# Dividing attention outputs ahead of the output weights instead of behind them, in a two-layer decoder on one core

## The reference, cut to what matters

```
attn = jax.nn.softmax(logits, axis=-1)
out = jnp.einsum('bhnm,bhme->bnhe', attn, v)
...
return jnp.dot(out, Wp) + bp
```

## Time and profile before

| | |
|---|---|
| median of 3 runs | 4618.46 us (4615.41 to 4620.7) |
| the profiled execution's own time, and its span | 4600.18 us, 4598.4 us |
| busy: PE, PEld | 4301.6 us (94%), 2382.7 us (52%) |
| busy: DVE, ACT, POOL | 2227.8 us (48%), 1803.9 us (39%), 3141.8 us (68%) |
| mean granted TensorE clock | 0.960 of 2.4 GHz |

### The profile page before, as it was taken

How to read it: one execution, slowest core, us unless ns; L and a number is a source line. 1 busy time by engine, 2 the same in 40 slices (tenths; PEclk the granted TensorE clock), 3 DMA queues, 4 the chain that set the end, 5 groups by cost and what they waited for, 6 DMA issues and landing times. The chain is left out here.

```text
span 4598.4 us, 69354 instructions
## 1 busy us (share of the span) xinstructions
PE 4301.6 (94%) x25904; PEld 2382.7 (52%) x25904; DVE 2227.8 (48%) x2764; ACT 1803.9 (39%) x2082; POOL 3141.8 (68%) x1379
## 2 busy tenths in 40 slices
PE   7999799999999999999999968599899999999968
PEld 3555455555555555555555446244455555555436
DVE  4555655555454555555455112456565545455212
ACT  2333244444444444444444422133234444444422
POOL 3556279989898988989899930000048989899950
PEclk9999899999999999999999979799779999999979
DMA  1000000000000000000000001100000000000001
GB/s 34 5 5 2 4 2 1 2 2 2 2 2 2 2 2 2 3 2 2 2 1 2 1 17 46 40 9 12 4 1 2 2 2 1 1 1 2 1 12 30
DMA packets 30387, 30.95 MB, mean 7 GB/s; under 512 B 6929, under 2 KB 22786, under 8 KB 30082
## 3 DMA queue, kind: packets, MB, share of 16 engines
q1 hardware_dynamic: 28626, 24.39, 1.8%
q10 hardware_dynamic: 1456, 2.46, 0.2%
HBM read 23.17 MB, written 3.67 MB: 6 GB/s over the span
## 5 line engine op out<-in xcount | busy, mean ns | idle before, releaser
L410 POOL TENSOR_TENSOR c_SUM<-c_SUM,c_PR 128x1024 f32<-128x1024 f32 (+1 forms) x1176 | 2792.9, 2375 | 263.9 <-ACT c_PR L490 158.7
L568 DVE TENSOR_REDUCE c_MX<-c_XB 128x2 f32<-128x1024 f32 (+2 forms) x1156 | 1394.3, 1206 | 1224.0 <-PE c_XB L690 1223.0
L490 ACT ACTIVATE c_PR<-c_S 128x1024 f32<-128x1024 f32 (+1 forms) x1224 | 1194.7, 1023 | 1694.9 <-PE c_S L735 1579.8
L753 PE MATMUL c_O<-c_PR,c_V 128*64 128x512 f32 (+1 forms) x4896 | 1197.0, 607 | 2.8 <-ACT c_PR L490 2.8
L753 PEld LDWEIGHTS c_O<-c_PR,c_V 128*64 128x64 f32 (+1 forms) x4896 | 294.0, 136 | 568.4 <-issue 394.1
L735 PE MATMUL c_S<-c_SH,c_ONE 64*128 64x512 f32 x2448 | 482.0, 389 | 0.0
L490 ACT ACTIVATE a_PR<-a_S 128x1024 f32<-128x1024 f32 x256 | 248.7, 1022 | 444.9 <-PE a_S L735 444.9
L568 DVE TENSOR_REDUCE a_MX<-a_XB 128x2 f32<-128x1024 f32 x246 | 301.2, 1224 | 188.0 <-PE a_XB L690 96.6
L690 PE MATMUL c_XB<-c_KHM,c_QH 64*128 64x512 f32 x1632 | 369.5, 448 | 11.7 <-DVE c_MX L568 7.7
L735 PE MATMUL c_S<-c_QH,c_KHM 64*128 64x512 f32 x1728 | 348.3, 399 | 8.5 <-ACT c_PR L490 8.4
L735 PE MATMUL c_S<-c_QH,c_KLM 64*128 64x512 f32 x1728 | 341.5, 391 | 0.0
(11 more groups left out here) (209 smaller groups left out, 4352.7 us busy)
## 6 DMA issues: line engine op xcount, KB each, us to landing
f_W<-in_L_w SPq DMA_DIRECT2D x34, 256.0 KB, 2.7
CTX<-in_ctx ACTq DMA_DIRECT2D x12, 192.0 KB, 4.4
a_KS<-scratch_k SPq DMA_DIRECT2D x16, 96.0 KB
a_QS<-scratch_q SPq DMA_DIRECT2D x16, 96.0 KB
scratch_q<-rot_qh SPq DMA_DIRECT2D x2, 512.0 KB, 4.6
scratch_k<-rot_kh SPq DMA_DIRECT2D x2, 512.0 KB, 6.2
c_WQ<-in_L_xattn_Wq SPq DMA_DIRECT2D x12, 64.0 KB, 1.8
c_WO<-in_L_xattn_Wo SPq DMA_DIRECT2D x12, 64.0 KB, 1.8
```

The lines of the kernel that those rows point to most:

```text
L410: pool.tensor_tensor(out[0:kp], out[0:kp], tile[0:kp], ALU.add).then_inc(summed, 1)
L490: act.activation(PR[u % BUFS][0:kp, :, :].rearrange("p h q -> p (h q)"), S[u % 2][0:kp, :], ACT.Exp)\
L568: dve.tensor_reduce(MX[:, q:q + tiles, :, column], bank[:].rearrange("p (h k) -> p h k", h=2) [:, :, 0:tiles * m].rearrange("p h (q k) -> ...
L753: last = pe.matmul(O[ROWS[h], :], V[pair.par][0:kp, t, ROWS[h]], PR[u % BUFS][0:kp, h, :], start=t == 0, stop=t == TILES - 1)
```

## The change

D is now made in the layout of the outputs, in which each partition is one dimension of one head and each column a query: the product of a block of ones with SUM gives every one of the head's 64 partitions the sum of its 512 queries (128x512 in all; in a1 one product with a matrix that has ones in the two rows that hold denominators). VectorE takes the reciprocal of all 512 columns, in four quarters of 128 columns (`divide`, two quarters in D's own group and two in the next), and multiplies OT with it in place (`normalise`). Y is then one job for both heads: four products over all 128 rows, and one addition of 128x512 to X. M is made with the transposing form of the product. In a0, K of the second chunk and Q move behind D; the tables keep Y two groups or more behind D.

```diff
-                g = 2
-                for job in [("D", 1 - half), ("YA", 1 - half), ("YB", 1 - half)] + jobs:
+                for job, g in [(("D", 1 - half), 2), (("Y", 1 - half), 5)] + [(job, 2) for job in jobs]:
...
-                self.side[half] = {(2, 0): ("D", 1 - half), (2, 1): ("YA", 1 - half), (3, 0): ("YB", 1 - half),
-                                   (3, 1): ("M", 1 - half)}
+                self.side[half] = {(1, 0): ("D", 1 - half), (3, 0): ("Y", 1 - half), (3, 1): ("M", 1 - half)}
...
-            self.side[0] = {(0, 0): ("Q", 0), (0, 1): ("K", 0), (1, 0): ("K", 1), (1, 1): ("D", 1), (2, 0): ("YA", 1),
-                            (2, 1): ("YB", 1), (3, 0): ("Q", 1), (3, 1): ("M", 1)}
-            self.side[1] = {(0, 0): ("V", 0), (1, 0): ("V", 1), (1, 1): ("D", 0), (2, 0): ("YA", 0), (2, 1): ("YB", 0),
-                            (3, 1): ("M", 0)}
+            self.side[0] = {(0, 0): ("Q", 0), (0, 1): ("K", 0), (1, 0): ("D", 1), (2, 0): ("K", 1), (2, 1): ("Q", 1),
+                            (3, 0): ("Y", 1), (3, 1): ("M", 1)}
+            self.side[1] = {(0, 0): ("V", 0), (1, 0): ("D", 0), (2, 0): ("V", 1), (3, 0): ("Y", 0), (3, 1): ("M", 0)}
...
+        self.division = [{job: at for at, job in side.items()}["D", 1 - half][0] for half, side in enumerate(self.side)]
...
-        RDEN = sb("RDEN", [P, 8])
+        RDEN = sb("RDEN", [P, HALF])
...
-                def output(half, ps, h, n):
+                def output(half, n):
 
                     dve.wait_ge(side_free, n)
-                    last = None
-                    for t in range(4):
-                        xt = X[:, 4 * half + t, :]
-                        last = dve.scalar_tensor_tensor(xt, ps[:, t * D:(t + 1) * D], RDEN[:, 2 * t + h:2 * t + h + 1],
-                                                        xt, ALU.mult, ALU.add)
-                    last.then_inc(side_free, 1)
+                    xt = X[:, 4 * half:4 * half + 4, :].rearrange("p t d -> p (t d)")
+                    dve.tensor_tensor(xt, SIDE[:], xt, ALU.add).then_inc(side_free, 1)
+
+                def divide(pair, half, parts, end=False):
+
+                    n = plan.job(pair.p, ("D", half), end)
+                    for i in parts:
+                        if i == 0:
+                            dve.wait_ge(side_done, n + 1)
+                        q = slice(i * P, (i + 1) * P)
...
+                        each = dve.reciprocal(RDEN[:, q], SIDE[:, q])
+                        if i == 3:
+                            each.then_inc(side_free, 1)
+
+                def normalise(pair, half, end=False):
...
+                    dve.wait_ge(side_free, plan.job(pair.p, ("D", half), end) + 1)
+                    dve.wait_ge(evac, 2 * to.p + half + 1)
+                    dve.tensor_tensor(OT[:], OT[:], RDEN[:], ALU.mult).then_inc(normal, 1)
...
-                        dve.reciprocal(RDEN[:], SIDE[:, 0:8]).then_inc(side_free, 1)
...
+                            after = group - plan.division[half]
                             maxima(0)
+                            if after == 1:
+                                divide(pair, 1 - half, (2, 3), end)
                             if group == GROUPS - 1 and not (end and half):
                                 shift(plan.maximum(pair.p, half, plan.half_maxima))
                             maxima(1)
+                            if after == 0:
+                                divide(pair, 1 - half, (0, 1), end)
+                            if after == 1:
+                                normalise(pair, 1 - half, end)
                             for job in side_jobs(half, group, 0, end):
...
                 def denominators(half):
+
+                    if packed is not None:
+                        return pe.matmul(SIDE[:], ones[:], OT[:], start=True, stop=True)
+                    last = None
+                    for h in range(2):
+                        last = pe.matmul(SIDE[ROWS[h], :], ones[:, ROWS[h]], SUM[half][:, h, :], start=True, stop=True)
+                    return last
+
+                def outputs():
                     last = None
                     for t in range(4):
-                        q = slice(t * P, (t + 1) * P)
-                        if packed is not None:
-                            last = pe.matmul(SIDE[:, 2 * t:2 * t + 2], OT[:, q], ones[:], start=True, stop=True)
-                            continue
-                        for h in range(2):
-                            last = pe.matmul(SIDE[:, 2 * t + h:2 * t + h + 1], SUM[half][:, h, q], ones[:, 0:1],
-                                             start=True, stop=True)
-                    return last
-
-                def outputs(h):
-                    last = None
-                    for t in range(4):
-                        last = pe.matmul(SIDE[:, t * D:(t + 1) * D], OT[ROWS[h], t * P:(t + 1) * P], WO[ROWS[h], :],
-                                         start=True, stop=True)
+                        last = pe.matmul(SIDE[:, t * D:(t + 1) * D], OT[:, t * P:(t + 1) * P], WO[:], start=True, stop=True)
                     return last
...
-                            last = pe.matmul(SIDE[:, t * P:(t + 1) * P], NM[:, t, :, :].rearrange("p h e -> p (h e)"),
-                                             ident[:], start=True, stop=True)
+                            last = pe.transpose(SIDE[:, t * P:(t + 1) * P], NM[:, t, :, :].rearrange("p h e -> p (h e)"),
+                                                ident[:])
...
-                        pe.wait_ge(evac, 2 * to.p + job[1] + 1)
+                        pe.wait_ge(normal, 2 * to.p + job[1] + 1)
```

More of the change, by code:

```diff
@@ L234, in of_pair @@
                 return pair.next()
-            return pair.back() if job[0] in ("D", "YA", "YB") and job[1] == 1 else pair
+            return pair.back() if job[0] in "DY" and job[1] == 1 else pair
         def absent(pair, job):
-            return pair is not None and pair.first and job[0] in ("D", "YA", "YB") and job[1] == 1
+            return pair is not None and pair.first and job[0] in "DY" and job[1] == 1
         def side_jobs(half, group, place, end):
@@ L334, in period @@
                     if not pair.first:
-                        sp.wait_ge(side_done, plan.job(pair.p, ("YB", 1)) + 1)
+                        sp.wait_ge(side_done, plan.job(pair.p, ("Y", 1)) + 1)
                         load_o(pair.p)
@@ L356, in _ @@
                 period(pair_at(pairs - 2), False)
-                sp.wait_ge(side_done, plan.job(pairs - 1, ("YB", 1), True) + 1)
+                sp.wait_ge(side_done, plan.job(pairs - 1, ("Y", 1), True) + 1)
                 load_o(pairs - 1)
@@ L535, in side @@
                     to = of_pair(pair, job)
-                    if kind == "V":
+                    if kind in "VD":
                         return
@@ L561, in side @@
                             dve.wait_ge(bias_added, 1)
-                        output(job[1], SIDE, "YA YB".split().index(kind), n)
+                        output(job[1], n)
                 def maximum(n, bank, unit):
@@ L605, in _ @@
                 dve.wait_ge(side_done, n + 1)
-                dve.reciprocal(RDEN[:], SIDE[:, 0:8]).then_inc(side_free, 1)
-                for h in range(2):
-                    dve.wait_ge(side_done, n + 2 + h)
-                    output(1, SIDE, h, n + 1 + h)
+                dve.reciprocal(RDEN[:], SIDE[:]).then_inc(side_free, 1)
+                dve.wait_ge(side_free, n + 1)
+                dve.wait_ge(evac, 2 * pairs)
+                dve.tensor_tensor(OT[:], OT[:], RDEN[:], ALU.mult).then_inc(normal, 1)
+                dve.wait_ge(side_done, n + 2)
+                output(1, n + 1)
             @block.tensor
@@ L814, in _ @@
                 pe.wait_ge(wo_in, 16 * pairs)
-                for h in range(2):
-                    pe.wait_ge(side_free, n + 1 + h)
-                    outputs(h).then_inc(side_done, 1)
+                pe.wait_ge(normal, 2 * pairs)
+                pe.wait_ge(side_free, n + 1)
+                outputs().then_inc(side_done, 1)
 class NormSemaphores:
```

28 lines of the change are left out of this document (19 added, 9 removed).

## The result

The changed kernel takes 4536.84 us (median of 4 runs, 4533.21 to 4538.78), the kernel before 4617.07 us in the same comparison: a ratio of 0.9824 with a 95% interval of 0.9807 to 0.9841, or 80 us less. The prediction was 4562 us, with a range of 4515 to 4610 us.

The account below looks back on a forecast made before the run. TensorE's own work, and every wait given to it, was taken as the bound. Gains of 15 us (c0, c1), 27 (a0), 13 (a1) and none at the ends, together 56, gave 4618.46 - 56 = 4562 us, range 4515 to 4610.

Parts of the forecast that it names:

- D: On TensorE, two overlapping products of 0.93 us replace sixteen short instructions of 1.87 us: 0.94 us gained a half pass.
- M: On TensorE, four transposing instructions replace eight at about 0.11 us each: 0.44 us gained a half pass.
- Y: On TensorE, one job of 1.08 us replaces YA and YB: gain 0.78 us in a0 and a1, 0.68 in c0 and c1.
- The reciprocal: On VectorE, 6.1 ns a column: 0.94 us a quarter, 3.3 us for all 512 columns.
- The dear case: Rival: reciprocal 1.16 us or more a quarter, SIDE's stall 1.8 us; 24 us gained, 4594 us. Chance 0.17.
- the cheap one: Rival: reciprocal 0.34 us a quarter, no SIDE stall beyond 0.1, none on XB; 119 us gained, 4499 us. Chance 0.14.
- The stall on SIDE: The next V or K behind D in c0, c1 and a0 waits 1.2 us for the reciprocal, 1.3 with the restart.
- XB in a1: Group 3's maximum product in a1 waits 0.8 us; net 0.9 us gained each, 15 times, 13 us.
- a0: First halves (K, Q) gain 2.1 us each, second halves (V) 1.5, the last 2 us: together 27 us.
- The ends: At the four ends, where nothing is beside, c0's 10.4 us from D to last addition becomes about 10: no change.
- The base: The profiled execution of the kernel before, 4600.18 us, is 18 us below the runs' median, so 4618.46 us was the base.
- the falls would come with each stall: Rival: TensorE's clock falls to 1.2 GHz in each new stall, 3.4 us each, 170 us lost, 4732 us. Chance 0.05.

Follow-up runs that it names:

- run 8: D's two products made twice in a row in a0, c0 and c1 of the changed kernel: 4546.77 us, ratio to the kernel before 0.987.
- run 2: The changed kernel with M made by products with the identity again, eight instructions in place of four: 4534.47 us, ratio to the kernel before 0.9836.
- run 11: The kernel of run 10 with M made by products with the identity: 4534.75 us, ratio to the kernel before 0.9828.
- late V: The changed kernel with V behind D one place later in c0 and c1 (K was not moved): 4530.55 us, ratio to the kernel before 0.9828.
- run 4: The changed kernel with plain copies in place of the reciprocal's quarters in the loops, leaving out the division: 4495.97 us, ratio to the kernel before 0.9751.
- run 9: The changed kernel with the reciprocal's quarters spread over VectorE's free slots, and D, V and K moved: 4606.38 us, ratio to the kernel before 0.9987.
- run 3: The kernel before with M's transposes as the only edit: 4588.61 us against 4609.72, ratio 0.9944.
- run 1: The kernel before, unedited, with a second profile: 4616.94 us, ratio 1.0; the profiled execution took 4617.98 us.
- run 12: The changed kernel with a copy of RDEN into OT in place of the multiplication in the loops: 4520.53 us, ratio to the kernel before 0.9801.
- run 6: The changed kernel with V behind D one place later in c0 and c1, and K or V ahead of D in a0: 4522.51 us, ratio to before 0.9813.
- run 10: The kernel of run 6 with a1's reciprocal quarters spread two, one, one: 4508.21 us, ratio to the kernel before 0.9778.

## Why the prediction was right, and where its sizes were off

- **D.** Predicted 0.93 us for two heads, a gain of 0.94. The trace has 0.91, doubling it costs 0.86 to 0.89 in three kinds of half pass (run 8). Shown. a1's D took 1.06 as against 1.
- **M.** Predicted 0.44 us a half pass. Undoing it costs 0.5 in every kind of half pass (runs 2 and 11), some 27 us over all of them; M holds TensorE for 0.59 us in place of 1.09. The Trainium skill's factor of four for FP32 (TensorE: Matmul & The Clock Gate, Terms) would make it 0.66 by the prediction's 0.11 us an instruction; the chip did half the instructions of the same length.
- **Y.** Predicted 1.08 us, a gain of 0.68 in c0 and c1; it held TensorE for 1.09. Read from the trace, not tested by itself.
- **The reciprocal.** Predicted 0.94 us a quarter and 3.3 for 512 columns; 0.89 to 0.96 and 3.36. The dear case is out, and so is the cheap one: the 512 columns took 6.6 ns each with all that is fixed. The Trainium skill's repeat count of 8 (VectorE: DVE Perf Modes, First, the fixed hardware budget), read as eight cycles a column at 0.96 GHz, would be 8.3 ns, an estimate from that page; the measurement does not bear out this reading.
- **The stall on SIDE.** This is the term that was mis-sized. "It now waits 1.2 us" and 1.3 with the restart; in the V halves of c0 it was 0.98, and taking it away gave 0.85 (late V) or 0.6 to 1.1 us (copies). The restart was not there: V's row is 1.15 us behind the wait and 1.16 without one. Counted from D's end (1085.60), the job was due at 4.4 us, as predicted, but the last quarter ended at 5.27 in place of 5.55, because two quarters take 1.76 us together. With the terms as measured a V half comes out right: 0.96 (D) + 0.67 (Y) + 0.50 (M) - 0.98 = 1.15 us, against 1.1. In the K halves the 0.91 us stall costs nearly nothing by itself: run 4 took it away and gained 0.1 us, because K's low part then holds the maximum product for 0.8 us. The prediction named a late reader of SIDE ("SIDE's next reader is pushed late enough to hold the maximum product behind it") as what would make it wrong. In the changed kernel it is just not that late: no wait for it shows in a K half of c0. That both halves gained the same 1.1 us is in part luck, since the wait that would take the stall's place had no term.
- **XB in a1.** Predicted 0.8 us; it was 0.38, and worth 0.44 (runs 4 and 9). Half passes gained 1.35 in place of 0.9, 20 us in place of 13.
- **a0.** Predicted 1.5 (V) and 2.1 (K, Q); it was 2.2 and 2.4. The new waits were 0.91 us for K and 0.73 for Q (1.3 and 0.6 predicted) and 0.93 for V (1.3). Some 0.2 us of the rest are not assigned to a term. Besides, four short falls of the clock in a0 before (half passes of 30.9, 30.7 and 30.7 us where 29.1 is usual, and one of 27.9 where 26.3 is) did not occur after: 6.5 us that no term had. They were also absent with M's transposes alone (run 3) and in run 2, so no single edit is shown to be the cause.
- **Sum.** Predicted 27 + 15 + 13 us; the stages gave 40, 13 and 20. In c0 and c1 the 1.1 us would be 22; the two half passes at the turns of c0's loop took 16.5 us more than usual, 10.4 of them in the four stops and the rest at a lower clock, where before's took 5.6, with 3.5 in two stops. The prediction read its price of a fall of the clock, 3.4 us, from the first of these two; 1.7 of it is a stop for which the profile names nothing.
- **The ends.** Predicted no change; c0's took 10.4 us from D to the last addition and takes 9.0 now, though the clock is low in both.
- **The base.** The profile of before was treated as 18 us below the median for all stages alike. It was one stretch, c0's lead, with a mean clock of 0.86 where run 1 has 0.60; the changed kernel's profile has 0.63. That the falls would come with each stall was rightly given little; that a stretch without any edit moves by 10 to 13.5 us with the clock was not foreseen.

The prediction was short by 24 us of the timed 80. Between run 1's profile and after's it is 26 of 82: 14 in a0 (6.5 of them its falls of the clock), 7 in a1, 7 in c0's lead, and c0 and c1 together 2 the other way, some 10 us more by the sizes of the terms and 12 lost at the loop's turns. So the mechanism held, and the time came out as near as it did partly because errors of both signs met. Open: what decides whether a lead runs at 1.2 or 2.4 GHz, and what TensorE stops for at the loop's turns.

## What to carry to other kernels

When a stall is removed, read the half pass (or whatever repeats), not the total: here a unit of work repeats within 0.1 us, while the total moves by up to 16 us with the clock in one lead, most of it a stretch that nobody edited; both leads together hid most of an edit of 27 us. Before paying for the removal of a wait, look for the second one behind the same engine; a copy in place of the slow instruction shows it in one run. A free slot on VectorE is free only for instructions that end before the next due reduction, and a multiplication or copy between SBUF tiles that meets a GpSimd addition ends only when that addition has: price it by what is left of that addition. A place where an addition is about to end should be the cheap one; no run moved the multiplication alone.

## What the hardware showed beyond that

- **VectorE beside GpSimd.** OT's multiplication of 512 columns, SBUF to SBUF, took 0.675 us in a1, where GpSimd is idle, 1.20 in a0 and 1.32 in c0, where it adds, up to 2.28 (2.77 in run 9). A plain copy went from 0.411 to 0.94 and 1.08. The addition of SIDE to X, with one operand from PSUM, took 0.69 us beside the same additions. The front's rows had no SBUF to SBUF instruction beside GpSimd, so the prediction used 0.69. The lengths follow a rule that the traces show: GpSimd's additions that were under way at 1091.86 (after) and at 1260.82 (run 9), when the multiplications shown above start, are

```profile
1090.45 2.35 POOL L412 TENSOR_TENSOR c_SUM<-c_SUM,c_PR 128x1024 f32<-128x1024 f32 x1
```

```profile
1260.57 2.39 POOL L413 TENSOR_TENSOR c_SUM<-c_SUM,c_PR 128x1024 f32<-128x1024 f32 x1
```

  They end at 1092.80 and 1262.96, and the multiplications 0.55 us later, at 1093.34 and 1263.52. So do all 22 multiplications of the half passes of c0 and c1 in after, in run 4 and in run 9, 0.55 to 0.58 us behind the end of the addition that they met; run 12's copies end 0.28 to 0.31 us behind it. The multiplication is not slowed by a factor, it waits for the addition to end. GpSimd's next addition, which starts while the multiplication still runs, takes 2.6 to 2.7 us in place of 2.35. This is why run 4 gained only 0.1 us in the K halves, and why the slots of run 9, which put the multiplication at the start of an addition, cost so much.
- **Two levels of a stretch.** c0's lead took 118 to 121 us with a mean clock of 0.84 to 0.87 (runs 2, 4, 8, 12 and the first profile of before), 129 to 137 at 0.59 to 0.63 in the others; c1's 113.5 to 114.0 (runs 2, 4, 6, 9, 10) or 124 to 127. The kernel before was seen with both. The edits differ in the leads only in the end of the self-attention and in M.
- **Stops at a loop's turn.** At the first half pass of the second and third turn of c0's loop TensorE stops for 1.5 to 3.1 us, 3.5 to 7.7 us into it, in all 14 profiles, once or twice, while the profile shows nothing that it waits for. c1's loop has one turn and none of these stops. What it is was not tested.
